# Criss-cross attention on one core: splits of the first batch two chunks ahead, three kinds of loads reordered

## The reference

```python
q = einsum('oc,bchw->bohw', Wq, x) + bq          # 64 channels
k = einsum('oc,bchw->bohw', Wk, x) + bk
v = einsum('oc,bchw->bohw', Wv, x) + bv          # 512 channels
energy_H = einsum('bchw,bcgw->bhwg', q, k) - 1e30 * eye[None, :, None, :]   # along a column
energy_W = einsum('bchw,bchv->bhwv', q, k)                                  # along a row
att = softmax(concatenate([energy_H, energy_W], -1), -1)
out = gamma * (einsum('bcgw,bhwg->bchw', v, att[..., :96])
             + einsum('bchv,bhwv->bchw', v, att[..., 96:])) + x
```

## Time and profile before

| | |
|---|---|
| median of 3 runs | 4036.08 us (4032.39 to 4038.2) |
| the profiled execution, its own time | 4029.24 us |
| its span, first to last instruction | 4027.5 us |
| TensorE busy | 3864.0 us (96%), granted clock 0.981 on average |
| DVE, ACT, POOL busy | 2433.0, 1663.7, 627.1 us |
| DMA queue of SP | 869.67 MB, 70.2% of 16 engines |

### The profile page before, as it was taken

One profiled execution on the slowest core, in us unless ns is written; L12 is line 12 of the kernel. 1 busy time (PEld: TensorE's weight loads), 2 busy tenths in 40 slices (PEclk: granted clock), 3 DMA queues, 4 the chain that ended last, 5 costly groups with the idle time before them and its releaser, 6 DMA issues.

```text
span 4027.5 us, 72644 instructions
## 1 busy us (share of the span) xinstructions
PE 3864.0 (96%) x28440; PEld 3830.9 (95%) x28440; DVE 2433.0 (60%) x5084; ACT 1663.7 (41%) x3658; POOL 627.1 (16%) x793
## 2 busy tenths in 40 slices
PE   5679999999999999999999999999999999999999
PEld 5579999999999999999999999999999999999999
DVE  4544668456674577745676466754668457673554
ACT  4442445424454244433444334542445424444111
POOL 0131003210032001310023100221003210042000
PEclk7789999999999999999999999999999999999999
DMA  4277775967768776677767777687775877758665
GB/s 165 85 201 219 236 254 185 242 219 241 233 198 227 232 243 226 203 217 239 245 213 213 217 245 251 198 226 219 238 251 186 234 220 236 242 186 226 202 200 173
DMA packets 256803, 874.33 MB, mean 217 GB/s; under 512 B 34256, under 2 KB 108496, under 8 KB 256464
## 3 DMA queue, kind: packets, MB, share of 16 engines
q1 hardware_dynamic: 256464, 869.67, 70.2%
HBM read 661.92 MB, written 207.62 MB: 216 GB/s over the span
## 4 chain that ended last, share of the span: by engine, by line
PE 90%; DMA 4%; DVE 4%; issue 1%; ACT 0%; POOL 0%; SPq 0%; DVEq 0%; ACTq 0%; POOLq 0%
PE bank L910 39%; PE bank L898 17%; PE bank L879 14%; PE bank L828 11%; DMA Pe<-e_scratch 4%; PE bank L838 3%; PE bank L865 3%; PE bank L847 3%; DVE E L629 1%; DVE mx L624 1%; DVE Sx L610 1%; DVE zs L638 0%; POOL Pe L390 0%; DMA XA<-in_x 0%; DVE Sy L615 0%
## 5 line engine op out<-in xcount | busy, mean ns | idle before, releaser
L910 PE MATMUL bank<-Sy,Wv_hi 128*128 128x384 f32 x6144 | 1596.1, 340 | 11.9 <-DVE Sy L615 11.9
L910 PEld LDWEIGHTS bank<-Sy,Wv_hi 128*128 128x128 f32 x6144 | 1088.3, 188 | 13.1 <-issue 13.1
L910 PE MATMUL bank<-Sy,Wv_lo 128*128 128x384 f32 x3072 | 1029.1, 335 | 0.0
L695 DVE SCALAR_TENSOR_TENSOR Y<-bank,bv_sb,Y 128x384 f32<-128x384 f32 x768 | 472.0, 615 | 871.7 <-PE bank L910 871.2
L390 POOL TENSOR_TENSOR Pe<-Pe,F 96x384 f32<-96x384 f32 x384 | 321.6, 840 | 2681.6 <-DMA Pe<-e_scratch 2647.7
L898 PE MATMUL bank<-Pt,XT_r 128*128 128x96 f32 x6144 | 724.8, 275 | 8.0 <-ACT Y L505 6.2
L898 PEld LDWEIGHTS bank<-Pt,XT_r 128*128 128x128 f32 x6144 | 705.0, 192 | 10.7 <-issue 7.6
L516 ACT ACTIVATE Sy<-Y 128x768 fp32r<-128x768 f32 x384 | 303.0, 836 | 896.6 <-PE bank L910 861.8
L678 DVE COPY Y<-bank 128x96 f32<-128x96 f32 x1536 | 317.5, 320 | 493.4 <-PE bank L879 493.4
L910 PEld LDWEIGHTS bank<-Sy,Wv_lo 128*128 128x128 f32 x3072 | 577.1, 188 | 0.0
L505 ACT ACTIVATE Y<-bank 128x96 f32<-128x96 f32 x1536 | 321.5, 359 | 395.1 <-PE bank L879 395.1
(11 more groups left out here) (62 smaller groups left out, 3298.0 us busy)
## 6 DMA issues: line engine op xcount, KB each, us to landing
Y<-in_x SPq DMA_DIRECT2D x192, 768.0 KB, 6.0
XT_r<-in_x_row SPq DMA_DIRECT2D x384, 384.0 KB, 5.4
out<-Y SPq DMA_DIRECT2D x192, 768.0 KB, 3.6
XA<-in_x SPq DMA_DIRECT2D x180, 768.0 KB, 6.9
XT_r<-in_x_col SPq DMA_DIRECT2D x192, 384.0 KB, 5.1
XT_c<-in_x_col SPq DMA_DIRECT2D x192, 384.0 KB, 5.1
e_scratch<-E SPq DMA_DIRECT2D x384, 144.0 KB, 2.7
Pe<-e_scratch SPq DMA_DIRECT2D x384, 144.0 KB, 7.0
```

What stands on the lines that cost most here:

```text
L695: nc.vector.scalar_tensor_tensor(at, proj_ps[c % 2][:, 0:CP], bv_sb[:, c:c + 1], at, op0=ALU.add, op1=ALU.add).then_inc(out_made, 1)
L910: last = nc.tensor.matmul(proj_ps[c % 2][:, 0:CP], w[:, ct, at], Sy[:, lo, ct, :], start=(ct == 0 and k == 0), stop=(ct == CT - 1 and k == 2))
```

## The change

Five edits. (1) In the prologue the split of chunk m + 2 is issued where that of m + 1 was: on ACT after the eviction of chunk m instead of ahead of it, on DVE ahead of the shift of chunk m; two splits are made before the loop. (2) The first three pieces of x for the first column stage are loaded in the row part's last steps (m = 20 to 22), and its first three P's after column group 8 instead of 12. (3) In the column stage, P of group g + 4 is loaded at the head of group g, where before P of g + 3 was (from g = 1 on); the first P beyond the stage moves from the row stage's start into the last group. (4) The residual's first chunk is loaded in the row stage behind piece 3 of x instead of in the middle of the column stage. (5) In row step n = 5 the DVE half of the next batch's first split comes after part 0 of the output instead of after part 2.

```diff
--- before.py
+++ after.py
@@ -262,8 +262,9 @@
                     .then_inc(out_stored[n % 2], 16)
 
             def first_loads(b):
-                for i in range(RRING):
-                    load_xtc(b, i)
+                if b:
+                    for i in range(RRING):
+                        load_xtc(b, i)
                 for i in range(PRING):
                     load_p(b, i)
 
@@ -273,19 +274,16 @@
                 for i in range(RRING + 1, CRING):
                     load_xtc(b, i)
                 for g in range(CHUNKS):
-                    if g:
-                        load_p(b, g + PRING)
+                    load_p(b, g + PRING + 1)
                     for i in (2 * g + CRING, 2 * g + CRING + 1):
                         if i < PIECES:
                             load_xtc(b, i)
                         elif i < PIECES + RRING:
                             load_xtr(b, i - PIECES)
-                    if g == CHUNKS // 2:
-                        load_xres(b, 0)
 
             def row_stage(b, more):
-                load_p(b, CHUNKS + 3)
                 load_xtr(b, 3)
+                load_xres(b, 0)
                 load_xtr(b, 4)
                 load_p(b, CHUNKS + 4)
                 load_xtr(b, 5)
@@ -333,12 +331,14 @@
                 for m in range(CHUNKS):
                     if m + 4 < CHUNKS:
                         load_xa_first(m + 4)
+                    elif m + 4 < CHUNKS + RRING:
+                        load_xtc(0, m + 4 - CHUNKS)
                     if m:
                         store_row_energies(0, m - 1)
                 store_row_energies(0, CHUNKS - 1)
                 for g in range(CHUNKS):
                     store_column_energies(0, g)
-                    if g == CHUNKS // 2:
+                    if g == CHUNKS // 3:
                         first_loads(0)
 
             def whole(b):
@@ -572,11 +572,12 @@
                 act.wait_ge(wqk_in, 16)
                 nc.scalar.activation(Wqk_hi[:, :, :], raw_qk[:, :, :], ACT.Copy).then_inc(w_hi_made, 1)
                 round_x(0, 0)
+                round_x(0, 1)
                 act.wait_ge(small_in, 48)
                 for m in range(CHUNKS):
-                    if m + 1 < CHUNKS:
-                        round_x(0, m + 1)
                     evict_kq(0, m, before=False)
+                    if m + 2 < CHUNKS:
+                        round_x(0, m + 2)
                     if m:
                         exponentials(0, m - 1)
                 exponentials(0, CHUNKS - 1)
@@ -719,6 +720,8 @@
                     b_now = b_groups(n) if more else []
                     turn_now = more and n == CHUNKS - 1
                     finish(b, n, 0)
+                    if more and n + 1 == A_FIRST:
+                        low_x(b + 1, 0)
                     if b_now and b_now[0]:
                         sum_z(b + 1, CHUNKS + b_now[0] - 1)
                     if a_now:
@@ -742,8 +745,6 @@
                         if a_now[1] + 1 < CHUNKS:
                             low_x(b + 1, a_now[1] + 1)
                         shift(b + 1, a_now[1])
-                    if more and n + 1 == A_FIRST:
-                        low_x(b + 1, 0)
                     if b_now:
                         shift(b + 1, CHUNKS + b_now[2])
                         sum_z(b + 1, CHUNKS + b_now[1])
@@ -775,9 +776,10 @@
                 nc.vector.tensor_tensor(Wqk_lo[:, :, :], raw_qk[:, :, :], Wqk_hi[:, :, :].bitcast(F32),
                                         ALU.subtract).then_inc(w_lo_made, 1)
                 low_x(0, 0)
+                low_x(0, 1)
                 for m in range(CHUNKS):
-                    if m + 1 < CHUNKS:
-                        low_x(0, m + 1)
+                    if m + 2 < CHUNKS:
+                        low_x(0, m + 2)
                     shift(0, m, before=False)
                     if m:
                         sum_z(0, m - 1)
```

## The result

The changed kernel takes 3886.4 us (median of 4, 3885.1 to 3887.74), the kernel before 4034.35: ratio 0.9632, 95% interval 0.9615 to 0.9649. The sign, the place of the gain and each mechanism came as forecast. Two sizes did not: the column stages' part, and the step from one profiled execution to the median.

The account below looks back on a forecast made before the run. TensorE fills the kernel, so only its idle and half-clock time can be won, most in the prologue's serial chain: -86 - 4 - 27 - 11 = -128 us, from the median 4036.08 to 3908 us, range 3894 to 3946.

Parts of the forecast that it names:

- What bounds the kernel: Whole kernel: TensorE busy 3864.0 of 4027.5 us; only 163 us idle and half-clock time can be won, mostly at prologue splits.
- Splits two chunks ahead: Prologue: DVE sets 3.40 us per chunk, last split at 86.8 instead of 171.08; -86 us, bounds -40 and -88.
- the signs: Prologue: last split near 87 us, DVE over 90% busy, clock near 1.00, TensorE's wait for the splits under 10 us.
- Which clock: Prologue: full clock despite 0.4 us gaps, as the profile row of its column part had 1.00 with gaps of 0.7.
- the rule on frequent micro-idles: Prologue: skill's rule that frequent micro-idles between matmul groups can make the clock oscillate; spoke against full clock.
- The loads keep up: Prologue: a chunk lands in 4.1 to 4.3 us, and three passes at 3.4 us leave 8.0 us for it.
- First loads: Start of first column stage: moved loads remove most of DVE's 4.44 us wait for a store; -4, bounds 0 and -4.4.
- P one group sooner: Column stages: earlier P and the residual's move remove stalls, -27 (bounds -5, -31), and their lost clock, -11 (-2, -13).
- The residual's move: Row stage: first chunk lands at 342 to 343, before its need at 344.23; 0, bounds 0 and +8.
- Edit 5: Row stage: TensorE had no wait at either place of the next batch's first split; 0, bounds -1 and +3.
- From the sum to the median: Whole kernel: -128 from the profiled 4029.24 us gives 3901; from the median 4036.08, 6.84 above, it gives 3908.
- The rivals: Clock alternates, 3930 (0.12); loads bound, 3920 to 3926 (0.10); stalls kept, 3939 (0.12); prologue slow, 3994 (0.02); residual late, 4050 (0.02).

Follow-up runs that it names:

- e10_no_sum: The changed kernel without the sums of the first batch's row exponentials in the prologue; 3885.52 us.
- e6_filler: The kernel before plus 12 unused matmuls ahead of each projection of the first batch from the third on; 4001.98 us against 4035.95.
- e5_splits: The kernel before with only the prologue's splits moved two chunks ahead, first loads as before; 3941.67 us, ratio 0.9775.
- e1_prologue: The kernel before with the splits two chunks ahead and the first column stage's loads moved; 91 us faster.
- e11_p_half: The changed kernel with P of group g + 4 issued behind the first x piece of group g instead of ahead of it; 3893.03 us.
- e7_low_x_back: The changed kernel with the next batch's first split put back after output 2; 3887.61 us.
- the second profile: The kernel before, unchanged, profiled a second time; 4032.55 us.
- e9_wv_late: The changed kernel with Wv's split moved on DVE behind the factors and the bias's scaling into an earlier DVE gap; 3885.1 us.

## Why the prediction was wrong, point by point

- **What bounds the kernel: right.** Serial chain in the prologue, P in the column stages, nothing in the row stages. Misread beside it: the other split buffer stood for 29.9 us of waits, not for as much again as 38.7.
- **Splits two chunks ahead, -86: right.** The pass is 3.32 us (3.40 was the sum of DVE's rows), set by DVE as e10_no_sum shows, the last split at 85.00 (86.8). The row part with Wv's split behind it ends 87.3 us sooner. Of the signs one failed: TensorE's waits for the splits are 15.3 us, not under 10, 9.3 of them the very first, which the change does not touch.
- **Which clock: right,** by the row and against the rule on frequent micro-idles that the prediction took from the Trainium skill: 1.00 in the passes with gaps of 0.3 us, 1.00 in e6_filler with gaps of 0.6. The rule may hold elsewhere; no run of gaps under 1 us did it here.
- **The loads keep up: right.** ACT never waited for XA in the steady passes; a chunk landed in 4.5 to 7.1 us against the 8.0 allowed.
- **First loads, -4: right,** 4 by e5_splits against e1_prologue.
- **P one group sooner, -27 with bounds -5 and -31, and -11 for the clock with bounds -2 and -13: the step that failed,** in size. It gave 50 in the pair of profiles, against 38. Added up from turn to turn (a group without a stall takes 3.91 us) in the kernel before, the 50 are: 30.9 of recorded waits, 4.2 by which the 20 groups with a wait grew beyond it, 14.8 in six groups at half clock, and 0.5 of other groups. So all the errors lie on one side. I kept back 0.5 us a batch for x piece 6, and nothing of it remained (4). I let 13 of 15.3 us of lost clock be felt and kept back 2 more; 14.8 were felt and none remained (4). And I priced a stall at its recorded wait, and called the sum of the recorded waits the bound, a term of 4 us put at nothing. It is no bound: a group of batch 1 with a wait recorded as 1.18 lasted 5.24 us from turn to turn (773.74 to 778.98), so it cost 1.33, and each of the 20 cost 0.15 to 0.53 more than recorded; e11_p_half shows it again (5.7 us for 4.0 recorded). The two turns in the trace of the kernel before:

```profile
773.74 0.49 PE L865 MATMUL bank<-ident,Pe 96*96 96x96 f32 x4
...
778.98 0.54 PE L865 MATMUL bank<-ident,Pe 96*96 96x96 f32 x4 [1.18 <-POOL Pe L390]
```

- **The residual's move, 0: right** for the row stage (landing 5.2 us, released by the projection). But the prediction gave it a share in removing the mid-stage stalls; with P sooner it has none.
- **Edit 5, 0: right** (e7_low_x_back).
- **From the sum to the median: the second step that failed.** I took the difference of 6.84 us between the profiled execution and the median as an offset that stays. 1.7 us of it were the median of only three runs. The other 5.1 went: the changed kernel's profiled execution lies 1.3 above its median, not below it. That the median execution had more of the stalls which the change removes fits the second profile (3.3 us longer in all, its column stages 6.1), but is argued from it and not shown. From the profiled execution's own time the forecast was 3901, and with 50 instead of 38 it is 3889.
- **The rivals:** none came. The clock stayed, loads were hidden, the full queue at the head of the column stages (1.04) was there and hurt nothing.

Open: why the stalls differ from execution to execution is not shown; the order in which the DMAs are issued is the same each time. Nor is it shown why batch 0's column stage is longer in the three kernels with another prologue and the old order of P. The prologue's 92 us and the 50 to 55 of the column stages make 142 to 147, against the timed 148. And e9_wv_late's 1.3 us were not timed beside the changed kernel.

## What to carry to other kernels

In a kernel that one engine fills to 96%, add up the stalls as the growth of a whole period (turn to turn here), not as the recorded waits: the waits miss the refill and the half clock behind them, here 50 us for 31 recorded, 15 of the difference half clock and 4 refill. Where timed runs of a kernel scatter much more than their neighbours (here 18 us against 3), the scatter may be a part of what can be won; profile it twice before a sum is made against one execution. Give a load that must not be late slack on the queue: here one period, ahead of the bulk loads, was enough and half a period was not quite; with it the bulk load that seemed to be the culprit could stay where it was. And before elementwise work is moved to an idle POOL, look at what DVE does beside it: 5.1 us of a subtraction on POOL cost 5.3 us of a split on DVE.

## What the runs showed of the hardware

Filling the gap of a serial chain with matmuls that nobody reads made the kernel 34 us faster: 140 us at clock 1.00 for the row part instead of 175 at 0.75. With gaps of 2.7 us in a pass of 5.7 to 8.2 the clock went to and fro between 1.2 and 2.4 GHz; with gaps of 0.3 or 0.6 in every pass it stayed at 2.4, and fell only behind the first gap of 2.8 us. POOL's 128 x 2048 subtraction took 5.12 us, and the half of DVE's two-input split that ran beside it took 5.29 us instead of 0.95; the other way round, POOL's scaling of P took 2.87 us instead of 0.82 beside a subtraction of DVE. In the column stages the DMA engines ran at 1.04 of their modelled capacity (270 GB/s) for 15 us without a single wait of TensorE.
